# An audio tower with a mixture of experts: six batches through sorted rows instead of five, on one core

## The reference

```python
gate_logits = jax.nn.relu(xf @ gw1 + gb1) @ gw2 + gb2
gate_weights = jax.nn.softmax(gate_logits, axis=-1)
top_w, top_idx = jax.lax.top_k(gate_weights, TOP_K)      # TOP_K = 2
top_w = jax.nn.softmax(top_w, axis=-1)
...
for e in range(E):                                        # E = 8
    h = jax.nn.gelu(xf @ we1[e] + be1[e], approximate=False)   # 128 -> 256
    y = h @ we2[e] + be2[e]                                     # 256 -> 128
    out = out + combine[:, e:e + 1] * y
```

## Time and profile before

| | |
|---|---|
| time, median of 3 runs | 224.91 us (224.11 to 225.05) |
| time of the profiled execution | 223.55 us |
| its span, first to last instruction | 221.8 us |
| PE / DVE / ACT / POOL busy | 93% / 70% / 62% / 51% of the span |
| mean granted TensorE clock | 0.996 of full speed |
| DMA: bytes moved, mean rate | 35.30 MB, 159 GB/s |

### The profile page before, as it was taken

How to read it: one execution, slowest core, us unless ns; L and a number is a source line. 1 busy time by engine, 2 the same in 40 slices (tenths; PEclk the granted TensorE clock), 3 DMA queues, 4 the chain that set the end, 5 groups by cost and what they waited for, 6 DMA issues and landing times.

```text
span 221.8 us, 5472 instructions
## 1 busy us (share of the span) xinstructions
PE 206.9 (93%) x1575; PEld 169.1 (76%) x1575; DVE 154.2 (70%) x688; ACT 136.9 (62%) x302; POOL 112.9 (51%) x168
## 2 busy tenths in 40 slices
PE   6997897899999999999999999999999889899990
PEld 6875656668957986798778876889998778699780
DVE  6169899999898998887788953486435333234895
ACT  2124987998889688867578447646645456444430
POOL 7626676720740055747674776005777676572000
PEclk9999999999999999999999999999999999999998
DMA  5999999950010003111211121377696899822673
GB/s 128 247 269 298 318 405 405 401 197 3 0 35 1 3 0 83 50 35 49 70 47 36 38 69 60 74 235 248 192 311 201 296 295 303 286 90 74 189 221 105
DMA packets 25856, 35.30 MB, mean 159 GB/s; under 512 B 4067, under 2 KB 18566, under 8 KB 25827
## 3 DMA queue, kind: packets, MB, share of 16 engines
q1 hardware_dynamic: 23137, 30.79, 43.7%
q0 software_dynamic: 2240, 4.00, 5.8%
q10 hardware_dynamic: 450, 0.16, 0.4%
HBM read 10.61 MB, written 14.39 MB: 113 GB/s over the span
## 4 chain that ended last, share of the span: by engine, by line
PE 73%; DVE 8%; SPq 6%; ACT 5%; issue 4%; DMA 2%; POOL 1%; DVEq 0%; ACTq 0%
PE PS L1188 11%; PE PS L1181 10%; PE PS L1123 7%; PE PS L1105 7%; PE PS L1213 5%; PE PS L1204 5%; PE PS L1000 5%; PE PS L988 4%; PE PS L1112 4%; SPq L444 3%; PE PS L1100 3%; SPq L436 2%; PE PS L1017 2%; DVE acc L964 2%; DMA blk_x<-xs 2%
## 5 line engine op out<-in xcount | busy, mean ns | idle before, releaser
L547 POOL DMA_INDIRECT ys<-yblk,blk_x x37 | 36.0, 972 | 27.5 <-DVE yblk L955 19.3
L517 POOL TENSOR_TENSOR rstd<-mv,mhalf 125x3 f32<-125x3 f32 x32 | 27.7, 866 | 42.3 <-DVE mv L697 42.0
L541 POOL DMA_INDIRECT xs<-rows_x,pos_x x30 | 29.9, 998 | 13.3 <-issue 8.4
L660 ACT ACTIVATE gd<-PS,bias 128x373 f32<-128x373 f32 x48 | 27.1, 574 | 15.4 <-PE PS L1181 10.7
L1181 PE MATMUL PS<-xt_sb,w_all 128*128 128x373 f32 x96 | 35.7, 482 | 0.0
L1188 PEld LDWEIGHTS PS<-w_all,gd 128*125 128x125 f32 x288 | 33.6, 188 | 2.1
L1188 PE MATMUL PS<-w_all,gd 128*125 128x128 f32 x288 | 34.6, 273 | 0.0
L671 ACT ACTIVATE gb_t<-PS,blk_w 128x128 f32<-128x128 f32 x58 | 18.0, 365 | 14.2 <-issue 7.7
L929 DVE SCALAR_TENSOR_TENSOR x_sb<-PS,comb,x_sb 125x128 f32<-125x128 f32 x72 | 20.7, 342 | 5.8 <-PE PS L1188 4.9
L1181 PEld LDWEIGHTS PS<-xt_sb,w_all 128*128 128x128 f32 x96 | 15.7, 190 | 5.0 <-issue 0.9
L955 DVE TENSOR_TENSOR yblk<-PS,blk_w 128x128 f32<-128x128 f32 x29 | 8.4, 290 | 14.9 <-PE PS L1213 14.5
(11 more groups left out here) (201 smaller groups left out, 414.1 us busy)
## 6 DMA issues: line engine op xcount, KB each, us to landing
blk_w<-w_all SPq DMA_DIRECT2D x29, 321.0 KB, 3.0
xs<-blank SPq DMA_DIRECT2D x1, 8256.0 KB, 25.8
blk_x<-xs SPq DMA_DIRECT2D x37, 64.5 KB, 3.2
yg<-ys SPq DMA_DIRECT2D x5, 336.0 KB
xt_sb<-in_xt SPq DMA_DIRECT2D x4, 375.0 KB, 5.9
x_sb<-in_x SPq DMA_DIRECT2D x4, 336.0 KB
out<-x_sb SPq DMA_DIRECT2D x8, 168.0 KB
w_all<-in_we SPq DMA_DIRECT2D x1, 1024.0 KB
```

The source lines that it names most:

```text
L517: pool.tensor_tensor(rstd[i][:, n % 2, :], mv[i][:, n % 2, :, 1], mhalf[:], ALU.pow)\
L541: pool.indirect_dma_start(xs, bass.IndirectOffsetOnAxis(ap=pos_x[:, b // 2, s, i:i + 1], axis=0), rows_x[:, k, s, j, :], None, bounds_chec ...
L547: pool.indirect_dma_start(ys, bass.IndirectOffsetOnAxis(ap=blk_x[n % SLOTS][:, t, D:XW].bitcast(u32), axis=0), yblk[n % YBUF][:, t, :], No ...
L660: act.activation(gd[:, k % GD, c, 0:TP], of("D1", n)[:, 0:TP], ACT.Gelu, bias=bias128[:, 2 + k % E * HC + c:3 + k % E * HC + c]).then_inc( ...
```

## The change

- Batch 0 becomes sparse: six sparse batches (0 to 5) and two dense ones (6 and 7). The number of blocks is computed from the 373 real tokens instead of 375: `NDYN` is 34 instead of 29, `NB` 42 instead of 37. Scatters are 36 instead of 30, block writes 42 instead of 37.
- `CAP` is 4096, and only the rows that can be read are blanked first (`FILL` = 21 blocks for each expert, in eight DMAs with `RI` = 7).
- `WSLOTS` is 14 instead of 7. The seven new weight buffers lie in the tensor `late`, which holds `prob` and `prob_t` during attention, so `lw.15` waits for the last attention product. `YBUF` is 12 instead of 6. Seven of the row buffers are the columns of `blank`.
- All `yl` are issued at once into six buffers, with no wait on a sum. Two of the six last sums (`fin.1`, `fin.3`) are scaled on ACT (`fm`) and added on POOL.
- The warm-up matmuls are 22, 13, 4, 3 and 1 instead of 12, 15, 5 and 3 (`WARM`).
- All five order tables are new. In the attention part no dense pieces are left; the 32 `D1` and 16 `D2` come after the last gate, between the blocks, and behind them. Some norms and copies change between ACT and DVE. SP issues ten `lw` ahead of `lx.0`, and POOL begins its scatters between the powers instead of after them.

The core of the diff; of the tables, one line stands for all:

```diff
-SPARSE = [1, 2, 3, 4, 5]
+SPARSE = [0, 1, 2, 3, 4, 5]
...
-NDYN = 2 * T * NS // BLK
+NDYN = (2 * TP * NS + E * (BLK - 1)) // BLK - E
 NB = E + NDYN
-MOST = -(-T * NS // BLK)
-CAP = 2048
+MOST = -(-TP * NS // BLK)
+CAP = 4096
...
-WSLOTS = 7
-YBUF = 6
+WSLOTS = 14
+OWN = 7
+YBUF = 12
...
-p4.6 scat.21 scat.22 p4.7 scat.23 scat.24 scat.25 scat.26 scat.27 scat.28 scat.29 so.0 so.1 so.2 so.3 so.4 so.5 so.6
+scat.20 scat.21 scat.22 scat.23 scat.24 scat.25 scat.26 scat.27 scat.28 p4.6 p4.7 scat.29 scat.30 scat.31 scat.32
...
-WARM = (12, 15, 5, 3)
+WARM = (22, 13, 4, 3, 1)
...
-        prob = sb("prob", [P, 2, NJ, TP])
+        late = sb("late", [128, (WSLOTS - OWN) * WROW])
+        prob = late[0:P, 0:2 * NJ * TP].rearrange("p (s j t) -> p s j t", s=2, j=NJ)
...
-            sp.dma_start(xs.rearrange("(q p r) d -> p q (r d)", p=128, r=RI),
-                         blank[:].rearrange("p r d -> p (r d)").unsqueeze(1).broadcast_to([128, PER // RI, RI * XW]))\
-                .then_inc(s_blank, 16)
+            for e in range(E):
+                sp.dma_start(xs[e * CAP:e * CAP + FILL * BLK, :].rearrange("(q p r) d -> p q (r d)", p=128, r=RI),
+                             blank[:].rearrange("p r d -> p (r d)").unsqueeze(1).broadcast_to([128, FILL // RI, RI * XW]))\
+                    .then_inc(s_blank, 16)
...
+                    if k == OWN:
+                        wait(sp, "at", B)
                     if k >= WSLOTS:
                         wait(sp, "yv", n + 1 - WSLOTS)
...
                 if name == "yl":
                     if n == 0:
                         for m in range(NB - YBUF, NB):
                             wait_so(sp, m)
-                    if n >= YG:
-                        wait(sp, "ob", n - YG + 1)
...
+                if name == "fin":
+
+                    k, b = RANK_POOL["fin", n], SPARSE[n]
+                    wait(pool, "fm", RANK_ACT["fm", n])
+                    pool.tensor_tensor(h2[:, b, :], h2[:, b, :], yg[n][:, 0, :], ALU.add).then_inc(S["obp"], 1)
+                    wait(pool, "obp", 2 * k - 1)
+                    pool.tensor_tensor(h2[:, b, :], h2[:, b, :], yg[n][:, 1, :], ALU.add).then_inc(S["obp"], 1)
...
+                if name == "fm":
+
+                    gathered(act, n)
+                    w = shares(n)
+                    for s in range(2):
+                        for j in range(NJ):
+                            last = act.activation(flat(yg[n][:, s, :])[j], flat(yg[n][:, s, :])[j], ACT.Copy,
+                                                  scale=w[:, s, j, :])
+                    last.then_inc(S["fm"], 1)
```

188 lines of the change are left out of this document (101 added, 87 removed).

## The result

The changed kernel takes **237.8 us** (median of 4 runs, 237.2 to 240.8) where the kernel before takes 225.0 beside it: ratio 1.058, 95% interval 1.053 to 1.064. The prediction was 227.3, slower, with a range up to 231.5. The sign was right, the size wrong by 10 us. The profiled execution took 238.28 us over a span of 236.4. Executions of one kernel fall into a faster and a slower group; medians here are of all of them, ratios and their intervals of the faster ones of both kernels.

The account below looks back on a forecast made before the run. It took PE, with DVE close behind, to bound the stretch before the table, and SP's queue the block stage. -0.5 + 3.1 - 0.2 = +2.4 us on the 221.8 span, scaled on the median: 227.3, range 220.5 to 231.5.

Parts of the forecast that it names:

- Attention up to the table: From 50 us until the table of blocks is ready: table at 119.9 us, between 115.6 and 124.4.
- POOL's path: POOL's scatters and powers from 78.2 us take 39.7 us; `p3.7` starts no earlier than 108.0, table 11.9 later.
- rival C: Before the table, POOL's first powers also wait for DVE: table at 124.4, +7.7 us, 232.7; chance 9%.
- rival D: PE's clock falls to its lower level, placed behind the last block: up to 240 us; chance 4%.
- the head: Longer first and shorter second warm-up ahead of the first convolution: +1.9 us, covered by nothing.
- Its floor: Earliest table by DVE's busy time with 5% idle: 115.6 us, 6.8 us earlier than now.
- rivals A and B: A: POOL's powers don't matter before the table, 222.6, 25%. B: dense work was the whole bound, 217.8, 9%.
- Table to first load: SP's 17 reads, 10 weight copies and one row copy take 18.9 us, for 16.9; first load at 138.8.
- First load to last block: SP's queue of loads, copies and reads bounds the block stage and takes 56.6 us: +3.1 us.
- stays 5.9: Time from SP's last weight copy to the end of PE's last block: unchanged at 5.9 us.
- Tail: From the last block on PE to the end: 22.9 us instead of 23.1.
- Gathers at once and two sums off DVE cost nothing and gain nothing here: Behind the last block these change nothing: DVE has 15.96 of 23.10 us and would wait for PE anyway.

Follow-up runs that it names:

- the fillers: Changed kernel with extra matmuls on the identity, results never read, in eleven places where PE waited: 235.2 us, ratio 1.048.
- the thinned one: Kernel before with early dense work cut to 16 columns on ACT and DVE, first-layer matmuls whole, second-layer pieces one matmul: 223.4 us, ratio 0.995.

## Why the prediction was wrong

Sum of the four terms: predicted +2.4, measured +14.6 us on the span.

*Attention up to the table* (predicted -2.45, measured +2.35; 119.9 and 124.7). Three things were off. First, POOL's path, which gave the 119.9: *"24 x 1.27 + 6 x 1.03 + 2 x 1.53 = 39.7"* has POOL begin at 78.2 and never wait, so `p3.7` at 108.0. At full clock, with the reads in a run, its first scatter began at 78.97, it waited 2.2 us for DVE's statistics, and `p3.7` started at 110.12; the table came 12.6 us later and not 11.9. That is 2.8 us. It is the mechanism of rival C at half its size, 2.2 of up to 4.5 us; that C's 124.4 hit the table's time is luck, for the rest was the clock.

Second, the clock, rival D: given 4% and put in the tail, it fell from 80 us on in the profiled execution and cost 2.0 us at the table by the versions that kept it, 2.6 by the fillers. The argument against it was that PE had 25.94 of 30 us busy without a fall; the changed kernel's stretches of 6.2 of 10 us had no counterpart there.

The third is *the head*, +1.9, which was +2.6, since ten more matmuls in the first warm-up took 3.1 us and not 2.4; the price came from the second warm-up, where they run faster. It was not hidden, as said. The first places were still ready at 77.5 to 78.0, near the assumed 78.2, so it adds nothing to the 4.8.

The bound under it, *"Its floor is therefore 50 + 1.9 + (63.28 - 2.8)/0.95 = 115.6 for the table"*, on which rivals A and B rest, took the stretch for one of capacity, and was never neared. Its load was wrong too: DVE's busy time hardly fell (63.03 at full clock, for 63.28), and PE's by 10 us, not 19.7. From the first places to the third the changed kernel needs 40.8 to 41.0 us at full clock (with fillers and without), the kernel before 41.0, the thinned one 39.5. So I read the stretch as a ring of waits over DVE, POOL, ACT and PE, with the dense work in its gaps: PE's 72.35 of 72.40 us looked like a bound, but fillers close a ring's gaps in the busy time as well. How much the dense work had lengthened the ring, and how much POOL's six more scatters lengthen it now, no run separates.

*Table to first load* (predicted +1.95, measured +4.45). The mechanism was right: SP's queue and not the scatters. The prices were not. The reads cost what was said, 0.61 for 0.63. But a copy cost 0.86 and not 0.70, since the price came from a copy with a load behind it and not from copies in a row: +1.6 us. The row copy cost 1.8 and not 1.2, and mixing reads and copies 0.6 where nothing stood.

*First load to last block* (predicted +3.1, measured +3.8). Right within a microsecond, and its two parts missed in opposite ways. To the end of the last copy it was 55.7 us for 56.6; the queue is the bound, as the loads put first show. From there to the last block, *"stays 5.9"*, it was 7.5: PE was busy for all of it at full clock, with 61 matmuls where the kernel before has 46.

*Tail* (predicted -0.2, measured +4.0). *"Gathers at once and two sums off DVE cost nothing and gain nothing here"* is the step that failed. PE's own work came out right, 19.3 us for 19.5 where its clock didn't fall (POOL's additions short). But DVE doesn't have free time where it is needed: in the kernel before it works without a pause from its first gathered sum to the end (207.4 to 219.3), and with all sums on DVE it ends 4.8 us after PE. So two sums off it should have been a gain, and POOL's additions beside it took 3.9 us back: DVE's sums slowed, PE waited 2.52 us, and its clock fell behind the wait. The share of 15.96 in 23.10 us is an average over a part where DVE waits and a part where it is the bound.

What the prediction said would show it right: SP with almost no wait from the table to the last copy, yes (2.7 us for free buffers, 77.2 us in all for "about 75"); POOL without a wait above 2 us and DVE waiting for `rstd`, yes (1.8 and 2.4 us); PE's busy time "about 53 us" before the table, no: 64.3, and 62.2 where the clock was 1.00 up to it; PE idle for 5 us or more between the blocks, no: 2.6.

## What to carry to other kernels

Before you count on an engine's free time, ask in which order it is needed: a stretch in which every engine is nearly full can still be a ring of waits, and busy times don't add up to its length. When you thin the filling to test that, check that the thinned engines really got free. Work taken out of such gaps can buy little, and where it was what kept PE busy, its clock can fall and take time; a busy share that stays high with fewer matmuls is the sign. Add up an engine's queue together with its waits for the others. Price queue items by the neighbours they will have. Before you move a sum to POOL, look for rows where both engines work at once. And when an edit moves a queue's items, list everything that it moves.
